# Softmax of a banded attention loop turned round: keys along the free axis, with six transposes, instead of sums and reciprocals by matmul

## What is computed

```python
x = x + 0.5 * ffn(layernorm(x))          # ffn(x) = x + expert[argmax(x @ gate_w.T)](x)
x = x + attn(layernorm(x))               # 16 heads of 64, window 128 to each side
x = x + 0.5 * ffn(layernorm(x))
# attn:
scores = einsum('bthd,bshd->bhts', q, k) * scale + bias    # bias: 0 in the band, -inf outside
attn   = softmax(scores, axis=-1)
out    = einsum('bhts,bshd->bthd', attn, v) @ Wout + bout
```

## Time and profile before

| | us |
|---|---|
| median of 3 runs | 2847.66 (2846.45 to 2865.02) |
| profiled execution | 2855.93 |
| its span on the slowest core (5) | 2854.4 |
| spans of the other cores | 2823.7 to 2849.8 |

### The profile page before, as it was taken

How to read it: one execution, slowest core, us unless ns; L and a number is a source line. 1 busy time by engine, 2 the same in 40 slices (tenths; PEclk the granted TensorE clock), 3 DMA queues, 4 the chain that set the end, 5 groups by cost and what they waited for, 6 DMA issues and landing times.

```text
span 2854.4 us, 30256 instructions; the slowest of 8 cores (2823.7 to 2854.4 us)
## 1 busy us (share of the span) xinstructions
PE 2185.9 (77%) x11152; PEld 1189.7 (42%) x11152; DVE 1083.0 (38%) x1832; ACT 311.2 (11%) x547; POOL 401.5 (14%) x512
## 2 busy tenths in 40 slices
PE   2776679899973877687777777677859699898983
PEld 0652224344461444334442444344439244343452
DVE  1112123333324544545454545454540323334332
ACT  2200000000001122112120212122140000000000
POOL 0000114142342000000000000000000011423433
PEclk9558889999996955685567656765565699999997
DMA  6008984554565410011001100000000255544565
GB/s 167 1 0 159 188 181 136 155 148 133 147 206 124 118 36 1 30 59 36 1 30 60 36 1 30 30 30 1 1 30 0 73 150 147 162 137 137 147 185 199
DMA packets 78158, 257.76 MB, mean 90 GB/s; under 512 B 9264, under 2 KB 20528, under 8 KB 73920
## 3 DMA queue, kind: packets, MB, share of 16 engines
q0 software_dynamic: 57680, 203.28, 27.1%
q1 hardware_dynamic: 20336, 52.55, 6.0%
HBM read 249.27 MB, written 33.63 MB: 99 GB/s over the span
## 4 chain that ended last, share of the span: by engine, by line
PE 70%; DMA 10%; DVE 8%; ACT 5%; issue 4%; SPq 1%; POOL 1%; DVEq 0%; ACTq 0%; POOLq 0%
PE pdf L93 30%; PE pss L93 9%; PE pst L93 8%; PE pq L93 5%; PE pgf L93 4%; ACT pn_bf_at L141 4%; DMA webuff<-wexp_bf 3%; PE pv L93 3%; DMA webuff<-wexpT 3%; PE pbf L93 2%; PE pso L93 2%; DMA wexp_bf<-webuff 2%; SPq L150 1%; PE pba L93 1%; DVE xc_at L104 1%
## 5 line engine op out<-in xcount | busy, mean ns | idle before, releaser
L93 PE MATMUL pdf<-lmbuff,webuff 128*128 128x512 bf16 (+1 forms) x5120 | 1050.6, 369 | 158.7 <-DVE lmbuff L104 78.9
L93 PEld LDWEIGHTS pdf<-lmbuff,webuff 128*128 128x128 bf16 x5120 | 510.5, 100 | 698.7 <-issue 224.6
L104 DVE TENSOR_TENSOR lmbuff<-xcf,mkbuff 128x1024 bf16<-128x1024 bf16 (+1 forms) x320 | 219.0, 693 | 692.7 <-PE pdf L93 679.3
L150 POOL DMA_DIRECT2D webuff<-wexp_bf x288 | 154.5, 537 | 1055.6 <-PE pdf L93 823.0
L146 DVE RECIPROCAL srow_at<-srow_at 1x256 f32<-1x256 f32 x128 | 222.9, 1741 | 13.2
L93 PE MATMUL pss<-biasq_sb,idb 128*128 128x128 bf16 x512 | 98.7, 296 | 164.4 <-ACT pn_bf_at L141 144.4
L141 ACT ACTIVATE pn_bf_at<-pss,negc_at 128x384 bf16<-128x384 f32 x256 | 134.5, 577 | 504.3 <-PE pso L93 447.7
L125 ACT CAST ev8f<-pdf 128x1024 bf16<-128x1024 f32 (+1 forms) x20 | 17.6, 930 | 1437.5 <-PE pdf L93 1437.5
L128 DVE COPY srow_at<-pst 1x256 f32<-1x256 f32 x128 | 52.6, 411 | 293.0 <-PE pst L93 293.0
L93 PE MATMUL pst<-srow_at,hmask_sb 1*128 1x128 f32 x512 | 155.6, 456 | 5.4 <-DVE tbuf_at L128 5.4
L93 PEld LDWEIGHTS pst<-srow_at,hmask_sb 1*128 1x128 f32 x512 | 118.1, 317 | 33.2 <-issue 33.2
(11 more groups left out here) (122 smaller groups left out, 1724.2 us busy)
## 6 DMA issues: line engine op xcount, KB each, us to landing
webuff<-wexp_bf POOLq DMA_DIRECT2D x288, 512.0 KB, 4.8
webuff<-wexpT POOLq DMA_DIRECT2D x32, 512.0 KB, 12.1
wexp_bf<-webuff SPq DMA_DIRECT2D x32, 512.0 KB, 10.2
wbufA_at<-wqkv_bf POOLq DMA_DIRECT2D x6, 2048.0 KB, 9.1
wbufB_at<-wqkv_bf POOLq DMA_DIRECT2D x6, 2048.0 KB, 8.2
x_sb<-xT SPq DMA_DIRECT2D x8, 1152.0 KB
mkbuff<-onehot_sc SPq DMA_DIRECT2D x64, 128.0 KB, 5.8
outT<-x_sb SPq DMA_DIRECT2D x8, 1024.0 KB, 12.9
```

The source lines that it names most:

```text
L93: E.matmul(a, b, c, start=st, stop=sp, tile_position=tp),
L104: eng, lambda E, o=out, x=a0, y=a1, op=op: E.tensor_tensor(o, x, y, op),
L150: eng, lambda E, o=out, i=in_: E.dma_start(o, i), inc=sem, n=16)
```

## The change

In the slot loop the scores are made the other way round: queries on partitions, 384 keys along the free axis. So a head's scores are one bias matmul and one matmul of Q by K, of 384 columns each, and the row sum comes out of the ACTIVATE itself (`accum_out`). DVE takes the reciprocal of a 128 x 2 tile and scales the exponentials, which are float32 now (`p32`, two buffers), into `pn_bf` (two buffers). For PV the keys must be on the partitions: PE transposes the six 128 x 128 blocks into PSUM (`ps_pt`, bfloat16), ACT copies them to `pt_sb` in one instruction of 128 x 768, and PE multiplies. ACT, no longer DVE, copies `ps_o` to `attnq4`. The sums by matmul, the copy and reciprocal of 1 x 256, the float32 matmuls, `tbuf` and the product are gone, and `hmask` with them. The pipeline is one iteration longer. The host lays the bias out for the new direction.

`produce_qk` has three buffers `pq` and `pw` in place of four. Each load of `x_sb` counts on a semaphore of its own (`dx0` to `dx7`), and the statistics of block k wait for that one alone; the gate's matmuls wait for it too. The order of the DMA issues on SP is as before.

```diff
     for k in range(KC):
-        b.dma("sp", "dsp", x_sb[:, k * T:(k + 1) * T], xT_d[k * 128:(k + 1) * 128, :])
+        b.dma("sp", f"dx{k}", x_sb[:, k * T:(k + 1) * T],
+              xT_d[k * 128:(k + 1) * 128, :])
...
-                    b.wait("dve", "dsp", init_sp)
-                    b.wait("act", "dsp", init_sp)
+                    b.wait("dve", f"dx{k}", 16)
+                    b.wait("act", f"dx{k}", 16)
...
                     for k in range(KC):
+                        b.wait("pe", f"dx{k}", 16)
                         b.mm(pg[:, tt * 8: tt * 8 + 8],
...
-                            if u >= 4:
-                                b.wait("pe", "act", Vc[u - 4])
+                            if u >= 3:
+                                b.wait("pe", "act", Vc[u - 3])
...
-                            if u >= 4:
-                                b.wait("pe", "dve", Rc[u - 4])
+                            if u >= 3:
+                                b.wait("pe", "dve", Rc[u - 3])
```

The slot loop after, one iteration (the waits and operations in the order in which they are emitted):

```diff
-                    for i in range(n + 7):
+                    for i in range(n + 8):
                         j = i - 2
                             b.wait("act", "pe", Acnt[j])
-                            if j >= 4:
-                                b.wait("act", "pe", Gcnt[j - 4])
+                            if j >= 2:
+                                b.wait("act", "dve", Dcnt[j - 2])
                             for jh in range(2):
                                 Ccnt[j] = b.actv(
-                                    pn_bf[:, s4 * 768 + jh * 384:
-                                          s4 * 768 + (jh + 1) * 384],
+                                    p32[:, pr * 768 + jh * 384:
+                                        pr * 768 + (jh + 1) * 384],
...
-                                    AF.Exp, bias=negc[:, 0:1], scale=0.125)
+                                    AF.Exp, bias=negc[:, 0:1],
+                                    scale=0.125,
+                                    accum=lr2[:, 2 * pr + jh:2 * pr + jh + 1])
...
                                 b.wait("pe", "act", Ccnt[i - 2])
...
+                                b.mm(ps_s[:, sb2: sb2 + 384], idb[:],
+                                     biasq_sb[:, bsel * 384:(bsel + 1) * 384],
+                                     True, False)
+                                Acnt[i] = b.mm(
+                                    ps_s[:, sb2: sb2 + 384],
+                                    q_sb[hb:hb + 64, hp * cfg.qown + qi * 128:
+                                         hp * cfg.qown + (qi + 1) * 128],
+                                    k_sb[hb:hb + 64, hp * R + qi * 128:
+                                         hp * R + qi * 128 + 384],
+                                    False, True)
                         j = i - 3
+                            b.wait("dve", "act", Ccnt[j])
+                            c = b.recip(rc2[:, 2 * pr:2 * pr + 2],
+                                        lr2[:, 2 * pr:2 * pr + 2])
+                            b.wait("dve", "dve", c)
                             if j >= 2:
+                                b.wait("dve", "pe", Ecnt[j - 2])
                             for jh in range(2):
+                                Dcnt[j] = b.ts(
+                                    "dve",
+                                    pn_bf[:, pr * 768 + jh * 384:
+                                          pr * 768 + (jh + 1) * 384],
+                                    p32[:, pr * 768 + jh * 384:
+                                        pr * 768 + (jh + 1) * 384],
+                                    rc2[:, 2 * pr + jh:2 * pr + jh + 1],
+                                    ALU.mult)
                         j = i - 4
+                            b.wait("pe", "dve", Dcnt[j])
                             if j >= 2:
+                                b.wait("pe", "act", Fcnt[j - 2])
+                            for kb in range(6):
+                                Ecnt[j] = b.tr(
+                                    ps_pt[pr][:, kb * 128:(kb + 1) * 128],
+                                    pn_bf[:, pr * 768 + kb * 128:
+                                          pr * 768 + (kb + 1) * 128],
+                                    idb[:])
                         j = i - 5
+                            b.wait("act", "pe", Ecnt[j])
                             if j >= 2:
+                                b.wait("act", "pe", Gcnt[j - 2])
+                            Fcnt[j] = b.cp("act",
+                                           pt_sb[:, pr * 768:(pr + 1) * 768],
+                                           ps_pt[pr][:])
+                        j = i - 6
+                            b.wait("pe", "act", Fcnt[j])
                             if j >= 2:
-                                b.wait("pe", "dve", Hcnt[j - 2])
+                                b.wait("pe", "act", Hcnt[j - 2])
                             # six PV matmuls, now from pt_sb
...
-                        j = i - 6
+                        j = i - 7
+                            b.wait("act", "pe", Gcnt[j])
+                            Hcnt[j] = b.cp(
+                                "act",
                                 attnq4[:, hp1 * qtw + qi1 * 128:
                                        hp1 * qtw + (qi1 + 1) * 128],
+                                ps_o[pr][:])
```

More of the change, by code:

```diff
@@ L634, in emit_attn @@
             rcolq = sb("rcolq", [128, nvt], F32)
-            pn_bf = sb("pn_bf", [128, 4 * 768], BF16)
-            srow = sb("srow", [1, 512], F32)
-            tbuf = sb("tbuf", [128, 256], F32)
+            p32 = sb("p32", [128, 2 * 768], F32)
+            pn_bf = sb("pn_bf", [128, 2 * 768], BF16)
+            pt_sb = sb("pt_sb", [128, 2 * 768], BF16)
+            nm2 = sb("nm2", [128, 4], F32)
+            nm2s = sb("nm2s", [128, 4], F32)
+            lr2 = sb("lr2", [128, 4], F32)
+            rc2 = sb("rc2", [128, 4], F32)
             negc = sb("negc", [128, 1], F32)
@@ L644, in produce_qk @@
                         nc.psum_tensor(f"pq{pp}{Q}{dst_w}", [128, 512], F32))
-                        for pp in range(4)]
+                        for pp in range(3)]
                     pw = [pscope.enter_context(
                         nc.psum_tensor(f"pw{pp}{Q}{dst_w}", [128, 512], F32))
-                        for pp in range(4)]
+                        for pp in range(3)]
                     wtens = wb[which][0]
@@ L832, in emit_attn @@
                     Acnt = [0] * n
+                    Bcnt = [0] * n
                     Ccnt = [0] * n
[L834 removed]
+                    Dcnt = [0] * n
                     Ecnt = [0] * n
[L836 to L837 removed]
+                    Fcnt = [0] * n
                     Gcnt = [0] * n
                     Hcnt = [0] * n
+                    Xd = [0] * n
                     def bsel_of(j):
@@ L923, in emit_attn @@
                             pr = j % 2
[L924 removed]
+                            b.wait("act", "pe", Ecnt[j])
                             if j >= 2:
[L926 to L933 removed]
+                                b.wait("act", "pe", Gcnt[j - 2])
[3 more added lines that the diff above has]
+                        j = i - 6
+                        if 0 <= j < n:
+                            pr = j % 2
                             qi1, hp1 = slots[j]
[L935 removed]
+                            b.wait("pe", "act", Fcnt[j])
                             if j >= 2:
[L937 removed]
+                                b.wait("pe", "act", Hcnt[j - 2])
                             for jh in range(2):
@@ L1075, in make_consts @@
         pswap[i, j] = 1.0
-    hmask = np.zeros((1, 256), dtype=np.float32)
-    hmask[0, 0:64] = 1.0
-    hmask[0, 128 + 64:256] = 1.0
-    return ident, pswap, hmask
+    return ident, pswap
 def make_band_bias(left_edge, right_edge):
@@ L1091, in make_band_bias @@
         last[:, 256:384] = NEG
-    blocks = []
-    for tile in (band, first, last):
-        for kb in range(3):
-            blocks.append(np.ascontiguousarray(
-                tile[:, kb * 128:(kb + 1) * 128].T))
-    out = np.ascontiguousarray(np.concatenate(blocks, axis=1))
+    out = np.ascontiguousarray(np.concatenate([band, first, last], axis=1))
     for v in range(3):
-        assert np.all(out[:, (v * 3 + 1) * 128: (v * 3 + 2) * 128] == 0.0)
+        assert np.all(out[:, v * 384 + 128: v * 384 + 256] == 0.0)
     return out
@@ L1143 @@
     wexpT = np.ascontiguousarray(wexp.transpose(0, 2, 1))
-    ident, pswap, hmask = make_consts()
+    ident, pswap = make_consts()
     B_, S, _ = x.shape
@@ L1156 @@
             "pswap": pswap, "crep": crep, "srep": srep, "biasq": biasq,
-            "hmask": hmask,
         })
```

91 lines of the change are left out of this document (12 added, 79 removed).

## The result

The changed kernel takes 2572.93 us (median of 10 runs, 2563.98 to 2581.36); the kernel before takes 2849.81 in the runs beside it (10 runs). The ratio is 0.9024, with a 95% interval of 0.9004 to 0.9043: 9.8% less, 277 us. The prediction was 2558 in a range of 2460 to 2680. Two of the ten runs before (2896 and 2904 us) and one of the four of experiment 2 (2630 us) fell in a slower state of the chip, and the ratios leave them out.

The account below looks back on a forecast made before the run. No engine is full; PE and ACT taking turns bound the slot loops. 2855.9 less 278 (four loops) less 12 (start) gave 2566 us for the profiled execution, 2558 for the median; range 2460 to 2680.

Parts of the forecast that it names:

- The turns: Slot loop: PE and ACT alternate now, 5.29 us a slot; the new order of waits ends this, giving 2.85.
- a ring over two slots: Slot loop: PE and ACT wait for each other in a round of two slots, 5.6 us or 2.8 a slot.
- The rival by which the turns go on slot by slot (2875): Slot loop: PE and ACT still alternate, 5.5 to 5.7 us a slot; chance 0.05, shared with something unseen.
- PE's sum: PE's work in a slot: scores 1.68, transposes 0.7 and PV 0.47 make 2.85 us, against 3.9 now.
- The loops' ends: Each slot loop's filling, about 12 us, and last slot's work, 8, beside 26 full slots.
- The transposes: PE, slot loop: six transposes of 128 columns overlap and cost 0.7 us a slot.
- The rival (2678): PE, slot loop: transposes do not overlap, cost 1.6 us, PE 3.8 a slot; chance 0.15, shared with a dear ACT accumulator.
- ACT: Slot loop: exponentials 1.06, accumulator output 0.3, copies 0.7 and 0.17 make 2.2 us a slot, against 1.06 now.
- DVE: Slot loop: two scalings at 0.35 (at most 0.6) and reciprocal 0.15, about 0.95 us a slot; not the bound.
- The clock: TensorE in slot loops stays at 0.50 (1.2 GHz); rival: it rises to 2.4 GHz, total 2478, chance 0.25.
- The start: Statistics wait for x, not gate weights: first copy of sums at about 45 us, 12 us less (7 to 14).
- The three buffers: Projections, `pq` and `pw`: one buffer less costs nothing; 66 us more if the cover were gone.

Follow-up runs that it names:

- experiment 2: Changed kernel with all x loads back on the one semaphore shared with the gate weights, statistics waiting for all of it: 2582.80 us, ratio 0.9052.
- experiment 6: Changed kernel without its two mask matmuls, so its output lacks the band: 2459.59 us, ratio 0.8636.
- experiment 7: Kernel of experiment 4 with the copy of `ps_o` on DVE, not ACT: 2437.40 us, ratio 0.8572.
- Experiment 1: Kernel before, with five buffers for the exponentials in place of four, so ACT waits for the PV of one slot earlier: 2696.39 us, ratio 0.9457.
- experiment 4: Changed kernel with both mask matmuls first, then both score matmuls, which then run side by side: 2466.81 us, ratio 0.8658.
- experiment 9: Kernel of experiment 4 with one more pair of score matmuls ahead, whose sums are overwritten: 2468.49 us, ratio 0.8677.
- number 10: Kernel of number 8 with the heads' score and mask matmuls one head behind the other again: 2515.93 us, ratio 0.8837.
- experiment 5: Changed kernel with plain identity matmuls (float32 output) in place of the transposes, half the weights wrong: 2564.17 us, ratio 0.9015.
- experiment 3: Changed kernel with four buffers `pq` and `pw` in `produce_qk` again, in place of three: 2570.28 us, ratio 0.9017.
- number 8: Kernel of experiment 7 with scores first, mask on the two outer key blocks only, and a third `pt_sb` buffer: 2438.02 us, ratio 0.8562.

## Why the prediction was right

**The turns.** It rested on the order of the waits: no wait of ACT on PE's own iteration, so a ring over two slots that is hidden behind PE. That held, and where PE is shorter the ring comes to light (experiments 6 and 7). In the changed kernel ACT's only long wait is the copy's for the PV of the iteration before, as it was put, and PE waits for no one. The rival by which the turns go on slot by slot (2875) is out by the chain alone. (Its own terms give 5.35 to 5.65 us a slot, not 5.5 to 5.7; nothing hangs on it.) Experiment 1 adds what the prediction had not separated: more than half of the gain comes from a wait that is one slot longer.

**PE's sum** was 2.85 us and is 2.95: scores 1.73 for 1.68 (each of four changes costs 0.11; one of them stands between PV and the first mask, both of 128 rows, where the columns of the array in use go from 64 to 128), transposes 0.76 for 0.70 (a fifth change, which the step did not count), PV 0.47 for 0.47. 0.1 us x 26 x 4 = 10 us is most of the 15 by which the forecast of 2558 was low; the other 5 are less than the FFN's scatter between cores, so a miss as small as this is in part luck. The loops' ends, put at 20 us, are 96.6 - 26 x 2.95 = 19.9.

**The transposes** were taken from the nearest row, the 128-column matmuls of 0.73 for six, against 1.6 from their durations. The row was right, and so was its reason, that durations overlap. The rival (2678) is out.

**ACT** was put at 2.2 us a slot and is busy 2.1. The accumulator's read has a row of 212 ns, above the 160 taken as the upper end, but only 0.10 of it lies between the starts of two instructions: 1232.94 to 1233.04, where the exponential ahead lasts to 1233.07. The pair with its reads is 1.25 (1232.47 to 1233.72), not 1.36. The copies came out as worked out from slope and fixed part: 801 and 274 ns for 0.80 and 0.27.

**DVE** took 417 ns for a scaling, between the 350 taken and the bound of 600, and 0.75 for two. Nothing hangs on it: DVE is busy 26.7 us of 96.6.

**The clock** was left at 0.50 with a chance of 0.25 for the rise. It stayed, as the reason given had it (bursts without a pause stayed at 0.50 already), though no run shows that this was the cause. Experiments 4, 9 and 10 show that the rival's time was only an order of four instructions away: it gave 2478 for the rise, and the kernels with it came at 2467 and 2468. That nearness is in part luck, since their slot is 1.99 us, or 2.1, where the rival had 2.25. What the prediction did not have is that the score matmuls of the two heads can run at the same time. The rule of the Trainium skill that it weighed there, on transposes, led to the right number, but experiment 5 shows the cause isn't theirs.

**The start** was put at a copy of the sums at 45 us; it is at 45.00, and the gain is 12 us in that stage (experiment 2). **The three buffers** cost nothing, as reckoned (experiment 3). **Behind the loop** nothing was taken back: outside the slot loops the attention takes 499.2 us on average over the cores, for 498.0, and the last stage lies within 4 us of what it was.

## What to carry to other kernels

Where two engines take turns and neither is full, look first at which slot's release the waiting engine needs: a buffer more, or work moved to another iteration, can bring as much as less work. Cost a run of short matmuls by the spacing of such a run in the trace, not by the mean duration of one, and add the cost of every change in the part of the array that they use; then put those that use different halves next to each other. And when the clock stands at its lower level with PE never idle, try the order of the matmuls before taking work out.

## What the runs showed of the hardware

- TensorE stayed at 1.2 GHz through whole loops in which PE was busy without a pause: 94.6 of 96.6 us in the changed kernel, 123.9 of 126.4 in experiment 1. In number 10 it stayed so for 81 us and more of a loop's 85.5. It went to 2.4 GHz in loops whose PE was busy less (53.0 of 69.7), but whose two 64-row matmuls ran side by side. Between numbers 8 and 10 the order of the matmuls is all that differs. Why the loop without masks stayed low is open.
- A change between matmuls of 128 rows and of 64 costs 0.11 us at 1.2 GHz on top of the columns (0.43 for 0.32), and so does the change from PV's matmuls to a mask (0.43 between their ends).
- A loop that is full on ACT hides a faster PE: from 2.41 us a slot at 1.2 GHz only 0.42 could be had by the doubled clock.
- An ACTIVATE with an accumulator output brings a second instruction of 212 ns, of which 0.10 us shows between starts.
